# Gathers held to TensorE's progress, and table high parts copied into PSUM, in a DLRM tower kernel on one core

## The chip, the core and the metric

The kernel runs on one core of a Trainium2 chip. The metric is the time of one execution on the device, in microseconds (us). Three runs of the kernel before took 646.27, 646.14 and 642.51 us: the median is 646.14 us.

## The reference, cut to what matters

For each of 2048 samples, 27 embedding rows of 128 floats are looked up, all pairs of them are multiplied, and 351 dot products and 16 dense inputs go through three small layers:

```python
e = jnp.stack([tbl_0[ids[:, 0]], ..., tbl_26[ids[:, 26]]], axis=1)      # 2048 x 27 x 128
dot = jnp.einsum('bnd,bmd->bnm', e, e)
z = dot.reshape(2048, 27 * 27)[:, pairs]                                  # 351 pairs
h = jnp.concatenate([z, dense_ctx], axis=1)
h = jnp.maximum(h @ W_top1 + b_top1, 0.0)                                 # 367 -> 512
h = jnp.maximum(h @ W_top2 + b_top2, 0.0)                                 # 512 -> 256
y = h @ W_top3                                                            # 256 -> 1
```

All is float32. Eight tables have 1000 rows, ten 1250, eight 12500 and one 125000.

## The kernel before, in words

The batch is cut into 16 tiles of 128 samples, and four tiles make a supertile (n = 0 to 3, t = 0 to 3; tile number k = 4n + t). Embedding rows come on two ways.

**Lookups.** Ten small tables ("hot", numbers h = 0 to 9, 84 chunks of 125 rows in all) lie in SBUF, split into a high part (`table_hi`, float32r) and a low part (`table_lo`, what is missing from the high part). VectorE makes a one-hot matrix for each chunk and 512 samples (L478), and TensorE multiplies the chunk's high and low part by it (L664, L666). It does so at the head of each supertile for all four tiles, in a ring of four one-hots, and counts each chunk in the semaphore `onehot_used`. An eleventh table (HALF) is looked up in the same way in supertiles 0 and 1 (L681, L682), and gathered in 2 and 3. In supertile 0 the tables also have to be made: ScalarE copies the raw table to `table_hi` (`split_high`, L527), VectorE subtracts it from the raw table into `table_lo` (`split_low`, L444), one table ahead of its one-hots, and ScalarE copies looked-up rows from PSUM to `eT` (L582), without which TensorE can't reuse the bank two tables later.

**Gathers.** The other 16 tables ("cold"; 17 in supertiles 2 and 3) are gathered by GpSimd (POOL) with one indirect DMA for each tile and table (L434, 128 rows of 512 bytes), 264 in all, in the order of the tiles. The rows of a tile go to one of three buffers, so the gathers of tile k wait, in groups of four tables, only until TensorE has transposed the same group of tile k - 3 (semaphore `transposed`).

**Tiles.** For each tile TensorE transposes the gathered rows group by group (L692), between the groups does layer 1 of the tile two back (L723), then layer 2 of the tile three back (L745), then the products of all pairs of the tile in four PSUM banks (L710, counted bank by bank in `dot_done`), with layer 3 (L766) between. VectorE and ScalarE copy transposed rows to `eT` (L494, L574) and products to `dots` (L231). SyncE stores them to DRAM and loads them back as pairs. All these matmuls are plain float32, and the trace has two records for each matmul of L710, L723 and L745; the lookups are float32r, with one record each.

Each engine works through its own list in the order of the code. Before the change `ps_tr` (2), `ps_dot` (2), `ps_h1` and `ps_h2` are six PSUM banks of their own.

Of the kernel before, what the change touches and what calls it, by code (L numbers as in the profile page):

```python
# [16 lines left out]
P = 128  # L17
BATCH = 2048
NF = 27
ST = 4  # L20
NS = BATCH // (ST * P)
# [8 lines left out]
NH, NC = len(HOT), len(COLD)  # L30
# [4 lines left out]
CR = 125  # L35
CHUNKS = [TABLE_ROWS[f] // CR for f in TABLES]
FROM = [sum(CHUNKS[:h]) for h in range(NT + 1)]
NCH = FROM[NH]
# [15 lines left out]
M1, M2 = H1 // P, H2 // P  # L54
# [4 lines left out]
SC = P // 2  # L59
WN = 2 * NF  # L60
SG = 32
BS = 8
NB_DOT = SG // BS
# [4 lines left out]
TG = 4  # L68
# [10 lines left out]
NHALF = 2  # L79
# [5 lines left out]
LAG2 = 3  # L85

STORED = 16 * (4 + 2)
assert ST == 4 and LAG1 < LAG2 < ST and NCH % NO == 0 and NH % 2 == 0 and NX == 10 and NGX == BACK + 1 == NG - 1


def pair_rows():
# [16 lines left out]
def dlrm_tower(nc, x):  # L108
    fp32, f32r, i32 = mybir.dt.float32, mybir.dt.float32r, mybir.dt.int32
# [3 lines left out]
    with ExitStack() as ctx:  # L113
# [3 lines left out]
        def ps(name, shape):  # L117
            return ctx.enter_context(nc.psum_tensor(name, shape, fp32))
# [8 lines left out]
        table_hi = sb("table_hi", [CR, FROM[NT], P], f32r)  # L127
        table_lo = sb("table_lo", [CR, FROM[NT], P], f32r)
# [23 lines left out]
        scratch = [nc.dram_tensor(f"dots_scratch{i}", (SR, P), fp32, kind="Internal").ap() for i in range(2)]  # L152

        ps_hot = [ps(f"ps_hot{i}", [P, ST * P]) for i in range(2)]
        ps_tr = [ps(f"ps_tr{i}", [P, TG, P]) for i in range(2)]
        ps_dot = [ps(f"ps_dot{i}", [P, ST * P]) for i in range(2)]
        ps_h1 = ps("ps_h1", [P, M1, P])
        ps_h2 = ps("ps_h2", [P, 4, P])


        last_h1 = [ps_hot[0][:, 0:P], ps_hot[1][:, 0:P], ps_tr[0][:, 0, :], ps_tr[1][:, 0, :]]
        last_h2 = [ps_dot[0][:, 0:P], ps_h1[:, 0, :]]
# [64 lines left out]
            return 2 * tile(n, t) + k // 2  # L227

        def copy_products(copy, i, k):
            of = banks[k][:, 0:BS * WN].rearrange("p (g w) -> p w g", w=WN)  # L230
            return copy(dots[i][:, :, BS * k:BS * k + BS], of)  # L231


        def gathered_before(n):
# [16 lines left out]
        def groups_through(n, g):  # L251
            return groups_before(n) + g + 1
# [28 lines left out]
        def splits(h, part=1):  # L281
            return part + 1 if h == 0 else h + 2

        def in_table(table, h, part):
            a, b = part_of(h, part)
            return table[:, FROM[h] + a:FROM[h] + b]
# [127 lines left out]
        @block.gpsimd  # L414
        def _(pool):
            pool.iota(row_number[:, 0, :], pattern=[[1, CH]], base=0, channel_multiplier=KINDS[0],
                      allow_small_or_imprecise_dtypes=True).then_inc(row_number_ready, 1)
            pool.iota(row_number[:, 1, :], pattern=[[1, CH]], base=0, channel_multiplier=KINDS[1],
                      allow_small_or_imprecise_dtypes=True).then_inc(row_number_ready, 1)
            pool.memset(ident[:, :], 0.0).then_inc(ident_zero, 1)  # L420
            pool.wait_ge(ident_zero, 1)
            pool.affine_select(out=ident[:, :], in_=ident[:, :], compare_op=ALU.not_equal, fill=1.0, base=0,
                               pattern=[[-1, P]], channel_multiplier=1).then_inc(ident_ready, 1)
            for k in range(NS * ST):
                n, t = k // ST, k % ST
                if k in (0, ST):
                    pool.wait_ge(cold_ids_ready[k // ST], 16)

                n0, t0 = (k - NR) // ST, (k - NR) % ST
                for f in range(NC if gathered(n) else NC - 1):  # L430
                    g = f // TG
                    if f % TG == 0 and n0 >= 0 and g < groups(n0):
                        pool.wait_ge(transposed[t0], groups_through(n0, g))
                    pool.indirect_dma_start(  # L434
                        out=rows[k % NR][:, f, :], out_offset=None, in_=x["cold"][f][:, :],
                        in_offset=bass.IndirectOffsetOnAxis(ap=cold_ids[:, k, f:f + 1], axis=0),
                    ).then_inc(rows_ready[t][g // BACK], 16)

        @block.vector
        def _(dve):  # L440
            def split_low(h, part=0):
                a, b = part_of(h, part)
                dve.wait_ge(hi_ready, splits(h, part))
                dve.tensor_tensor(in_table(table_lo, h, part), staging[h][:, a:b], in_table(table_hi, h, part),  # L444
                                  ALU.subtract).then_inc(lo_ready, 1)


# [58 lines left out]

            for i in range(2):
                dve.memset(zT[i][96:P, 1, :], 1.0).then_inc(cleared, 1)

            for i in range(2):  # L510
                dve.memset(ps_dot[i][:, :], 0.0).then_inc(cleared, 1)
            dve.wait_ge(row_number_ready, 2)
            supertile(0, first=True)
            for n in range(1, NS - 1):
# [8 lines left out]
        def _(act):  # L523
            def split_high(h, part=0):
                a, b = part_of(h, part)
                act.wait_ge(raw_ready[h] if h else first_ready[part], 32)
                act.copy(in_table(table_hi, h, part), staging[h][:, a:b]).then_inc(hi_ready, 1)  # L527

            def half_out(n, c):
                act.wait_ge(half_onehot_used, halves(n, c) + NX)  # L530
# [121 lines left out]
        def _(pe):  # L652
# [42 lines left out]
            def products(n, t, q, first):  # L695
                if q == 0:
# [2 lines left out]
                        pe.wait_ge(hot_read[pair], hot_uses(n + 1, pair))  # L699
                    if not gathered(n):  # L700
                        pe.wait_ge(half_read, 2 * n + t // 2 + 1)
                if first and t == 0 and q == 1:
                    pe.wait_ge(cleared, 4)
                for k in (2 * q, 2 * q + 1):
                    if not (first and t == 0):
                        pe.wait_ge(dot_read[k % 2], bank_reads(n, t, k) - 1)
# [146 lines left out]
```

## Time and profile before

| | |
|---|---|
| median of three runs | 646.14 us |
| the profiled execution, its time | 642.85 us |
| the profiled execution, its span (first to last instruction) | 641.0 us |
| TensorE busy, matmuls | 404.4 us (63%) |
| VectorE busy | 215.7 us (34%) |
| ScalarE busy | 97.9 us (15%) |
| GpSimd busy | 260.6 us (41%), 259.7 of it in 264 gathers |
| granted TensorE clock, mean | 0.787 of full speed |

The profile gives for every engine when it worked and what ended its waits. "issue" in it is time in which an engine waited for nothing that the profile shows, and "remote" is a release that the profile can't place. The stages of the span, read from the timeline: lookups of supertile 0 to about 60 us and its tiles to 194; lookups of supertile 1 to 235 and its tiles to 358; lookups of supertile 2 to 398 and its tiles to 521; lookups of supertile 3 to 561 and its tiles to 623; the rest is the end of the last tile's layers.

### The profile page before, as it was taken

Reading aid. Unit: us, or ns where it says so; the run is one execution under the profiler, and the core shown is the slowest. Engines: PE = TensorE matmul, PEld = TensorE weight load, DVE = VectorE, ACT = ScalarE, POOL = GpSimd, SP = SyncE. Lnnn points to the kernel's source line nnn. Section 1 sums busy time; section 2 is a strip of 40 time slices with the busy share of each in tenths; the row PEclk is TensorE's granted clock in tenths of the full one; section 3 lists DMA queues with packets and bytes.
Section 4 is the critical chain, followed back from the end, with each engine's and each line's share of the span. In section 5 each row is a group of like instructions: output and inputs, shape, how many; then the busy total and the mean of one; then the engine's idle time right before and its main releaser. Section 6 shows DMA issues by size and latency. Waiting matters only on the chain.

```text
span 641.0 us, 9183 instructions
## 1 busy us (share of the span) xinstructions
PE 404.4 (63%) x3768; PEld 341.8 (53%) x3768; DVE 215.7 (34%) x462; ACT 97.9 (15%) x190; POOL 260.6 (41%) x272
## 2 busy tenths in 40 slices
PE   5888315263739992819271999371808089955997
PEld 3667204152628891718161888261707078845996
DVE  6898003010109960301010797010101059801220
ACT  2442001010111210102020212010201012110322
POOL 6778763544540027363645001737273600072000
PEclk9899557585959996758685999666767579985999
DMA  8983313131414202223222230123232325010322
GB/s 224 248 213 93 82 49 69 49 81 38 97 37 91 61 13 53 55 67 62 61 62 60 49 103 8 50 44 86 39 84 45 77 34 114 9 50 23 59 48 36
DMA packets 71137, 45.23 MB, mean 71 GB/s; under 512 B 53100, under 2 KB 59628, under 8 KB 71096
## 3 DMA queue, kind: packets, MB, share of 16 engines
q1 hardware_dynamic: 60578, 25.80, 18.0%
q0 software_dynamic: 8448, 17.32, 10.7%
q10 hardware_dynamic: 2070, 1.53, 1.0%
q8 instruction: 30, 0.49, 0.3%
q14 instruction: 11, 0.09, 0.0%
HBM read 38.75 MB, written 5.87 MB: 70 GB/s over the span
## 4 chain that ended last, share of the span: by engine, by line
PE 54%; issue 33%; DVE 4%; another core or an unknown queue 3%; DMA 3%; SPq 1%; ACT 1%; ACTq 0%
PE ps_hot L710 12%; PE ps_hot L664 10%; PE ps_hot L666 9%; PE ps_h L723 6%; PE ps_dot L710 6%; PE ps_tr L692 5%; PE ps_h L745 3%; DVE onehot L478 3%; DMA dots<-in_tbl 2%; PE ps_h L766 2%; PE ps_hot L681 1%; PE ps_hot L682 1%; DVE table_lo L444 1%; DMA dots_scratch<-dots 1%
## 5 line engine op out<-in xcount | busy, mean ns | idle before, releaser
L434 POOL DMA_INDIRECT rows<-in_tbl,cold_ids x264 | 259.7, 984 | 320.6 <-PE ps_tr L692 237.9
L710 PE MATMUL ps_hot<-eT 128*54 128x54 f32 x1024 | 77.2, 261 | 214.7 <-issue 195.3
L710 PEld LDWEIGHTS ps_hot<-eT 128*54 128x54 f32 x1024 | 59.1, 171 | 232.5 <-issue 211.9
L478 DVE TENSOR_SCALAR onehot<-hot_ids,row_number 125x512 fp32r<-125x512 int32 x336 | 146.8, 485 | 4.7 <-PE ps_hot L666 2.6
L664 PE MATMUL ps_hot<-onehot,table_hi 125*128 125x512 f32 x336 | 134.2, 399 | 14.8 <-DVE onehot L478 10.9
L666 PE MATMUL ps_hot<-onehot,table_lo 125*128 125x512 f32 x336 | 132.9, 396 | 0.0
L231 DVE COPY dots<-ps_hot 128x432 f32<-128x432 f32 x16 | 9.7, 608 | 238.3 <-remote 131.7
L664 PEld LDWEIGHTS ps_hot<-onehot,table_hi 125*128 125x128 f32 x336 | 64.2, 191 | 33.1 <-issue 17.6
L666 PEld LDWEIGHTS ps_hot<-onehot,table_lo 125*128 125x128 f32 x336 | 64.2, 191 | 13.1
L494 DVE COPY eT<-ps_tr 128x512 f32<-128x512 f32 (+1 forms) x36 | 23.3, 648 | 111.6 <-remote 56.4
L723 PE MATMUL ps_h<-zT,w 128*128 128x128 f32 x360 | 50.6, 281 | 0.0
L723 PEld LDWEIGHTS ps_h<-zT,w 128*128 128x128 f32 x360 | 46.0, 197 | 0.1
L582 ACT COPY eT<-ps_hot 128x512 f32<-128x512 f32 x40 | 26.6, 665 | 107.0 <-PE ps_hot L666 107.0
L692 PE MATMUL ps_tr<-ident,rows 128*128 128x128 f32 x264 | 41.8, 280 | 0.9 <-ACT eT L574 0.7
L710 PEld LDWEIGHTS ps_dot<-eT 128*54 128x54 f32 x1024 | 37.4, 164 | 6.2 <-issue 6.1
L710 PE MATMUL ps_dot<-eT 128*54 128x54 f32 x1024 | 39.4, 249 | 1.2 <-issue 1.2
L544 ACT ACTIVATE h<-ps_h,b 128x128 f32<-128x128 f32 x30 | 9.4, 363 | 159.5 <-remote 146.8
L692 PEld LDWEIGHTS ps_tr<-ident,rows 128*128 128x128 f32 x264 | 31.3, 144 | 3.3 <-ACT eT L574 1.4
L574 ACT COPY eT<-ps_tr 128x512 f32<-128x512 f32 (+1 forms) x36 | 20.1, 559 | 65.0 <-remote 39.1
L745 PE MATMUL ps_h<-h,w 128*128 128x128 f32 x240 | 29.4, 276 | 0.4 <-ACT results L554 0.4
L745 PEld LDWEIGHTS ps_h<-h,w 128*128 128x128 f32 x240 | 28.0, 192 | 0.8 <-ACT h L539 0.7
L231 DVE COPY dots<-ps_dot 128x432 f32<-128x432 f32 x16 | 9.7, 608 | 44.4 <-PE ps_dot L710 44.4
(39 smaller groups left out, 140.0 us busy)
## 6 DMA issues: line engine op xcount, KB each, us to landing
hot_ids<-in_hot_ids SPq DMA_DIRECT2D x40, 256.0 KB
dots_scratch<-dots SPq DMA_DIRECT2D x62, 87.8 KB
rows<-in_tbl,cold_ids POOLq DMA_INDIRECT x264
zT<-dots_scratch SPq DMA_DIRECT2D x47, 58.5 KB
w<-in_tbl SPq DMA_DIRECT2D x3, 448.0 KB
dots<-in_tbl SPq DMA_DIRECT2D x2, 560.0 KB
dots<-in_tbl SPq DMA_DIRECT2D x2, 448.0 KB
w<-in_tbl SPq DMA_DIRECT2D x1, 560.0 KB
```

The costliest lines, as they stand in the source:

```text
L231: return copy(dots[i][:, :, BS * k:BS * k + BS], of)
L434: pool.indirect_dma_start(out=rows[k % NR][:, f, :], out_offset=None, in_=x["cold"][f][:, :], in_offset=bass.IndirectOffsetOnAxis(ap=cold_ ...
L478: dve.tensor_scalar(onehot[:, c % NO, :], hot_ids[h % NI][0:CR, :], row, None, ALU.is_equal).then_inc(onehot_ready, 1)
L494: dve.tensor_copy(eT[:, i, :, at:at + len(f), :], ps_tr[1][:, 0:len(f), :].rearrange("d f (q b) -> d q f b", b=2))\
L574: act.copy(eT[:, t % 2, :, at:at + len(f), :], ps_tr[0][:, 0:len(f), :].rearrange("d f (q b) -> d q f b", b=2)).then_inc(tr_read[0], 1)
L582: act.copy(eT[:, :, :, NC + h:NC + h + NH + 1:NH, :], ps_hot[h % 2][:, :].rearrange("d (a i q b) -> d i q a b", a=2, i=2, b=2))\
L664: pe.matmul(ps_hot[h % 2][:, :], table_hi[:, c, :], onehot[:, c % NO, :], start=(c == FROM[h]), stop=False)
L666: pe.matmul(ps_hot[h % 2][:, :], table_lo[:, c, :], onehot[:, c % NO, :], start=False, stop=(c == FROM[h + 1] - 1)).then_inc(onehot_used, 1)
L692: last = pe.transpose(ps_tr[pair][:, f - TG * g, :], rows[tile(n, t) % NR][:, f, :], ident[:, :])
L710: last = pe.matmul(banks[k][SC * c:SC * c + WN, WN * g:WN * g + WN], e.rearrange("d a b -> d (a b)"), e.rearrange("d a b -> d b a"), start ...
L723: last = pe.matmul(ps_h1[:, m, :], w1[0:k, c, m * P:(m + 1) * P], zT[i][0:k, c, :], start=(c == 0), stop=(c == KC - 1))
L745: last = pe.matmul(ps_h2[:, m, :], w2[:, c, m * P:(m + 1) * P], h1[:, c, :], start=(c == 0), stop=(c == M1 - 1))
```

## The change

**Gathers.** A planner, `within_reach`, runs before the program is built. It counts in steps, lets gathers follow each other at 3 steps each and TensorE do a chunk in 1 step (1.3 in supertile 0) and a tile in 23 (12 for the first two), and notes for every group of gathers how many chunks and how many product banks TensorE is planned to have finished 24 steps before the group begins. GpSimd then waits for that many (`onehot_used`, `dot_done`) ahead of the group, besides the wait for `transposed` that was there.

**PSUM.** For the tables 1 to 9 and the HALF table, ScalarE also copies the raw table, rounded in the same way, to three adjoining PSUM banks (`apart`), and `hi_ready` is counted only after that copy. VectorE's subtraction reads the high part there instead of in `table_hi`. From table 3 on ScalarE waits ahead of the copy until VectorE has subtracted the table two before, which had the same banks. For this the six banks become two tensors of three banks each. The two memsets of `ps_dot` and TensorE's wait for them go, and the copies of products read only the 118 partitions that are written.

```diff
+FIRST_CHUNK, HALF_STEPS, TILE_STEPS, FIRST_TILE, BANK_STEPS, GATHER_STEPS = 1.3, 5, 23, 12, 2, 3
+FIRST_LOOKUP, FIRST_GATHER, LANDING, LEAD = 15, 9, 5, 24
...
+def within_reach():
+    begun, landed = {}, []
+    step = FIRST_GATHER
+    for k in range(NS * ST):
+        for f in range(NC if k // ST >= NHALF else NC - 1):
+            begun.setdefault((k, f // TG), step)
+            step += GATHER_STEPS
+        landed.append(step + LANDING)
+    chunks, banks = [], []
+    step = FIRST_LOOKUP
+    for n in range(NS):
+        for c in range(NCH):
+            step += 1 if n else FIRST_CHUNK
+            chunks.append(step)
+        for t in range(ST):
+            if n < NHALF and t % 2 == 0:
+                step += HALF_STEPS
+            step = max(step, landed[ST * n + t]) + (FIRST_TILE if n == 0 and t < 2 else TILE_STEPS)
+            banks += [step - BANK_STEPS * (NB_DOT - 1 - b) for b in range(NB_DOT)]
+    return {at: [sum(done <= begin - LEAD for done in of) for of in (chunks, banks)] for at, begin in begun.items()}
...
+                    if f % TG == 0 and reach[k, g][0] > chunks_done:
+                        chunks_done = reach[k, g][0]
+                        pool.wait_ge(onehot_used, chunks_done)
+                    if f % TG == 0 and reach[k, g][1] > banks_done:
+                        banks_done = reach[k, g][1]
+                        pool.wait_ge(dot_done, banks_done)
...
-                dve.tensor_tensor(in_table(table_lo, h, part), staging[h][:, a:b], in_table(table_hi, h, part),
+                high = apart[h % 2][:, 0:CHUNKS[h]] if h else in_table(table_hi, h, part)
+                dve.tensor_tensor(in_table(table_lo, h, part), staging[h][:, a:b], high,
...
-                act.copy(in_table(table_hi, h, part), staging[h][:, a:b]).then_inc(hi_ready, 1)
+                high = act.copy(in_table(table_hi, h, part), staging[h][:, a:b])
+                if h:
+                    if h > 2:
+                        act.wait_ge(lo_ready, splits(h - 2))
+                    high = act.copy(apart[h % 2][:, 0:CHUNKS[h]].bitcast(f32r), staging[h])
+                high.then_inc(hi_ready, 1)
...
-            for i in range(2):
-                dve.memset(ps_dot[i][:, :], 0.0).then_inc(cleared, 1)
...
-                if first and t == 0 and q == 1:
-                    pe.wait_ge(cleared, 4)
```

What the planner gives, worked out from its code (chunk numbers within the supertile, 84 in each):

| group of gathers | waits for |
|---|---|
| tile 0 group 3, tiles 1 and 2, tile 3 group 0 | chunk 4 (13, 23, ... 78, 84) of supertile 0 |
| tile 3 groups 1, 2, 3 | 3rd bank of tile 0; 3rd, 4th bank of tile 1 |
| tile 4 groups 0, 1; tile 5 group 0 | 1st, 4th bank of tile 2; 2nd bank of tile 3 |
| tile 5 group 1 to tile 7 group 0 | chunk 8 (20, 32, ... 80, 84) of supertile 1 |
| tile 7 group 2; tile 8 groups 0, 2, 4; tile 9 group 0 | 4th bank of tiles 4, 5, 6; 2nd, 3rd bank of tile 7 |
| tile 9 group 1 to tile 10 group 3 | chunk 11 (23, 35, ... 74, 84) of supertile 2 |
| tile 11 groups 0 to 4; tile 12 groups 0, 1, 4; tile 13 group 0 | banks of tiles 8, 8, 9, 9, 10; 10, 10, 11; 11 |
| tile 13 group 1 to tile 14 group 3 | chunk 11 (23, ... 74, 84) of supertile 3 |
| tile 15 groups 0 to 4 | banks of tiles 12, 12, 13, 13, 14 |

GpSimd's list, at the gathers of the tiles 0 to 3 (each row is a gather or a run of them, with the semaphores that it waits for). Before, 48 gathers stand with no wait but that for the ids:

```order
L434 DMA rows<-in_tbl,cold_ids 128x128 [waits cold_ids_ready0]
L434 DMA rows<-in_tbl,cold_ids 128x128 x47
L434 DMA rows<-in_tbl,cold_ids 128x128 [waits transposed0]
L434 DMA rows<-in_tbl,cold_ids 128x128 x3
L434 DMA rows<-in_tbl,cold_ids 128x128 [waits transposed0]
```

Of the change, at the end of tile 2's gathers and in tile 3's and 4's:

```order
L474 DMA rows<-in_tbl,cold_ids 128x128 [waits onehot_used]
L474 DMA rows<-in_tbl,cold_ids 128x128 x3
L474 DMA rows<-in_tbl,cold_ids 128x128 [waits onehot_used,transposed0]
L474 DMA rows<-in_tbl,cold_ids 128x128 x3
L474 DMA rows<-in_tbl,cold_ids 128x128 [waits dot_done,transposed0]
L474 DMA rows<-in_tbl,cold_ids 128x128 x3
L474 DMA rows<-in_tbl,cold_ids 128x128 [waits dot_done,transposed0]
L474 DMA rows<-in_tbl,cold_ids 128x128 x3
L474 DMA rows<-in_tbl,cold_ids 128x128 [waits dot_done,transposed0]
L474 DMA rows<-in_tbl,cold_ids 128x128 x3
L474 DMA rows<-in_tbl,cold_ids 128x128 [waits dot_done,transposed1,cold_ids_ready1]
```

No gather has changed its place; from here on a group also waits for a chunk or for a bank of products.

ScalarE's list at the tables 2 to 5 in supertile 0, before:

```order
L527 CAST table_hi<-w 125x1024 [waits raw_ready2]
L527 CAST table_hi<-w 125x1024 [waits raw_ready3]
L582 COPY eT<-ps_hot 128x128x2x2 [waits onehot_used]
L527 CAST table_hi<-dots 125x1024 [waits raw_ready4]
L582 COPY eT<-ps_hot 128x128x2x2 [waits onehot_used]
```

And of the change, in which the tensors with names in `ps_tr_h` and `ps_dot_h` are the two threes of banks:

```order
L565 CAST table_hi<-w 125x1024 [waits raw_ready2]
L569 CAST ps_tr_h<-w 125x1024
L565 CAST table_hi<-w 125x1024 [waits raw_ready3]
L569 CAST ps_dot_h<-w 125x1024 [waits lo_ready]
L625 COPY eT<-ps_hot 128x128x2x2 [waits onehot_used]
L565 CAST table_hi<-dots 125x1024 [waits raw_ready4]
L569 CAST ps_tr_h<-dots 125x1024 [waits lo_ready]
L625 COPY eT<-ps_hot 128x128x2x2 [waits onehot_used]
```

Between a table's first copy and the next copy to `eT` there is now a second copy of the table's size.

## Rows read from the trace of the kernel before

**Rows 1.** The page's span in 40 slices, digits in tenths: GpSimd, granted clock.
```profile
POOL 6778763544540027363645001737273600072000
PEclk9899557585959996758685999666767579985999
```
**Rows 2.** Waits: engine, tile, line, releaser: us in total, times, longest.
```profile
POOL rows L434 <- PE ps_tr L692: 237.9, 12, 50.8
...
PEld ps_hot L710 <- issue: 211.9, 159, 16.5
```
**Rows 3.** Gathers (L434) by stretch: length, busy (count), PE clock, DMA share, GB/s.
```profile
11.00:58.00 47.00, 37.86 (x31) 0.96 0.80 193
62.00:194.00 132.00, 69.71 (x74) 0.64 0.27 65
194.00:235.00 41.00, 0.00 (x0) 1.00 0.25 59
236.00:358.00 122.00, 62.64 (x67) 0.71 0.24 57
...
398.00:521.00 123.00, 63.71 (x68) 0.67 0.24 57
...
561.00:591.00 30.00, 16.04 (x17) 0.66 0.14 38
592.00:623.00 31.00, 0.00 (x0) 1.00 0.31 56
```
**Rows 4.** Timeline (start, us, what) of TensorE in tiles 13 to 15.
```profile
599.72 1.88 PE L710 MATMUL ps_dot<-eT 128*54 128x54 f32 x64
...
601.53 0.66 PE L692 MATMUL ps_tr<-ident,rows 128*128 128x128 f32 x4
...
612.18 0.66 PE L692 MATMUL ps_tr<-ident,rows 128*128 128x128 f32 x4
```
**Rows 5.** Timeline of all engines in tile 9, while tile 12 is gathered.
```profile
428.14 0.94 POOL L434 DMA_INDIRECT rows<-in_tbl,cold_ids  x1 [9.68 <-PE ps_tr L692]
...
430.12 0.69 DVE L494 COPY eT<-ps_tr 128x512 f32<-128x512 f32 x1 [1.52 <-PE ps_tr L692]
...
434.91 0.59 ACT L574 COPY eT<-ps_tr 128x512 f32<-128x512 f32 x1 [5.30 <-remote]
...
445.25 0.29 DVE L494 COPY eT<-ps_tr 128x128 f32<-128x128 f32 x1 [14.43 <-remote]
...
448.11 0.94 POOL L434 DMA_INDIRECT rows<-in_tbl,cold_ids  x1 [0.30 <-issue]
...
456.16 2.74 PE L710 MATMUL ps_dot<-eT 128*54 128x54 f32 x64
```
**Rows 6.** Timeline in supertile 0's lookups, gathers running.
```profile
42.33 3.25 DVE L478 TENSOR_SCALAR onehot<-hot_ids,row_number 125x512 fp32r<-125x512 int32 x8
...
43.63 1.28 POOL L434 DMA_INDIRECT rows<-in_tbl,cold_ids  x1 [0.30 <-issue]
...
43.97 0.39 PE L664 MATMUL ps_hot<-onehot,table_hi 125*128 125x512 f32 x1
...
44.42 0.40 PE L664 MATMUL ps_hot<-onehot,table_hi 125*128 125x512 f32 x1
```
**Rows 7.** Supertile 2's lookups: length, PE, PEld, DVE, ACT, POOL busy, clock, DMA.
```profile
358.00:397.00 39.00, 38.64 (x175) 31.92 (x172) 36.91 (x84) 6.76 (x11) 0.00 (x0) 1.00 0.24 63
```
**Rows 8.** Timeline: a gather beside a subtraction of `split_low`.
```profile
11.62 2.41 POOL L434 DMA_INDIRECT rows<-in_tbl,cold_ids  x1 [0.30 <-issue]
...
11.91 1.22 DVE L444 TENSOR_TENSOR table_lo<-dots,table_hi 125x1024 fp32r<-125x1024 f32 x1
```
**Rows 9.** Timeline of ScalarE and TensorE at table 3 of supertile 0.
```profile
22.32 1.05 ACT L527 CAST table_hi<-dots 125x1024 fp32r<-125x1024 f32 x1 [4.45 <-DMA dots<-in_tbl]
23.27 0.61 ACT L582 COPY eT<-ps_hot 128x512 f32<-128x512 f32 x1
...
23.98 0.47 PE L664 MATMUL ps_hot<-onehot,table_hi 125*128 125x512 f32 x1 [1.86 <-ACT eT L582]
```

More of the change, by code:

```diff
@@ L154, in dlrm_tower @@
         ps_hot = [ps(f"ps_hot{i}", [P, ST * P]) for i in range(2)]
[L155 to L158, printed above, removed]
+        ps_tr_h1 = ps("ps_tr_h1", [P, 3, 4, P])
+        ps_dot_h2 = ps("ps_dot_h2", [P, 3, 4, P])
+        apart = [bank.rearrange("p a c d -> p (a c) d")[0:CR] for bank in (ps_tr_h1, ps_dot_h2)]
+        ps_tr = [ps_tr_h1[:, i] for i in range(2)]
+        ps_dot = [ps_dot_h2[:, i].rearrange("p c d -> p (c d)") for i in range(2)]
+        ps_h1 = ps_tr_h1[:, 2]
+        ps_h2 = ps_dot_h2[:, 2]
         last_h1 = [ps_hot[0][:, 0:P], ps_hot[1][:, 0:P], ps_tr[0][:, 0, :], ps_tr[1][:, 0, :]]
@@ L229, in copy_products @@
         def copy_products(copy, i, k):
-            of = banks[k][:, 0:BS * WN].rearrange("p (g w) -> p w g", w=WN)
-            return copy(dots[i][:, :, BS * k:BS * k + BS], of)
+            of = banks[k][0:SC + WN, 0:BS * WN].rearrange("p (g w) -> p w g", w=WN)
+            return copy(dots[i][0:SC + WN, :, BS * k:BS * k + BS], of)
         def gathered_before(n):
@@ L423, in _ @@
                                pattern=[[-1, P]], channel_multiplier=1).then_inc(ident_ready, 1)
+            reach = within_reach()
+            chunks_done = banks_done = 0
             for k in range(NS * ST):
```

## The prediction

> **What bounds the kernel now.** I read four views, in this order. The slices of the page first: GpSimd's gathers and the granted clock run against each other. Where GpSimd shows no digit, the clock is at 9 (2.4 GHz); where it shows 5 to 7, the clock is at 5 to 7, half of the slice at 1.2 GHz [rows 1]. The first slices are the exception, and matter below. Then the waits: TensorE's weight loads for the products sat idle for 211.9 us for nothing that the profile shows, and GpSimd sat idle for 237.9 us until TensorE had transposed [rows 2]. So neither is busy throughout, and each waits for the other. Third, the gathers by stretch: 74, 67, 68 and 17 of the 264 lie in the tile stages of the four supertiles, none in the lookups of supertiles 1 to 3, 38 (264 less these 226) ahead of tile 0 [rows 3]. With three row buffers, tile k's gathers can only start when tile k - 3 is being transposed, and then all 16 or 17 go out in one run.
>
> Last, single tiles. Tiles 13 to 15, with no gather left, follow each other at 612.18 - 601.53 = 10.65 us [rows 4]. The four tiles of supertile 2 took 123 us [rows 3], 30.8 each. What happens in between is seen in tile 9 [rows 5]: the first gather of the run goes out at 428.14, VectorE still gets its transposed rows at 430.12, but ScalarE gets the next ones only at 434.91 (5.3 us idle), VectorE the last at 445.25 (14.4 us idle), though TensorE's records for them lie far earlier. The last gather starts at 448.11, and the second half of the products then runs at its usual pace. So while gathers are under way TensorE's float32 work nearly stands still, and the tile stages cost four clean tiles plus a price per gather: (123 - 4 x 10.65) / 68 = 1.18 us, about the step at which gathers follow each other (0.94 + 0.30 us, rows 5). This is a correlation, with no cause that the trace shows; I take it as the mechanism since tile 12, which has gathers but no ids to load for a next supertile, also took 30 us [rows 3].
>
> The lookups don't suffer so. In supertile 0 gathers run all the time, and yet chunks follow at 44.42 - 43.97 = 0.45 us [rows 6], and 84 chunks at that step are the 39 us of a later lookup stage without gathers [rows 7]. Gathers under lookups are free, and gathers under tiles cost 1.18 us each. The span is set by how many lie where.
>
> The Trainium skill's page "SBUF — State Buffer", section "Who interferes with whom", says that TensorE never waits on anyone at SBUF and that DMA doesn't contend with a compute engine. By that rule the gathers are not the cause and moving them would bring nothing; the tiles with and without them, 30.8 against 10.65 us, speak against it here.
>
> **The gathers' new waits.** They move nothing in GpSimd's list but hold groups back, from tile 5 on, until TensorE is in its next lookups. Counting what fits there: gathers beside lookups follow at 47 / 31 = 1.52 us [rows 3]. Supertile 1: held until chunk 8, so 76 chunks of 0.455 us and a half lookup of 2.5 us (estimated from the chunk's step) are left, 37 us: 24 gathers. Supertiles 2 and 3: until chunk 11, 33 us: 22 each. The planner wants 28, 25 and 25; the rest runs over into the tiles. Ahead of tile 0 I put 41 instead of 38 (next part). That makes 109 under lookups and 155 under tiles, where there were 226: 71 fewer x 1.18 = **-84 us**. Behind a waiting gather only gathers are queued on GpSimd, and TensorE waits for them last. Tile 15's last group is held until the second bank of tile 14; it lands some us later, when tile 15 has its first three groups to do. I price that at 0 to 4 us, and at 0.
>
> Two costs stand against it. The last four tiles: before, 17 gathers were done in tile 12 and three tiles ran at the 2.4 GHz level. Now 22 and more are spread over tiles 12 to 14. The gathers are in the count, but the clock isn't: 64 records of products took 2.74 us after a stall and 1.88 at full clock [rows 4, 5]. Two such halves and a layer 2 of about 1.9 us more (estimated: twice its time at half the clock) are 3.6 us a tile, three tiles: **+11 us**. And the runs are broken up: some 20 instead of 13. A run's stall sets in 2 to 3 us after its first gather, and ends some 3 us after the last [rows 5], so each further run costs 0 to 1.2 us: **+2** of at most 9.
>
> **The PSUM part.** Per table one more ScalarE copy of 1.05 us, ahead of the copy to `eT` that TensorE waits for at table 3 [rows 9]: +1 us there and about +1 for VectorE's wait at table 2 (the same 1.05 us). Later ScalarE has the time: three copies are 2.8 us beside 4.5 us of VectorE per table (eight one-hots 3.25 and a subtraction 1.22, rows 6 and 8). **+2 us.** VectorE's subtraction with one operand in PSUM isn't in the trace. Its copies out of PSUM lie at 0.69 us for 512 elements [rows 5], the subtraction at 1.22 for 1024 [rows 8], per element 1.35 against 1.19 ns with the fixed part in it. So between nothing and 10 x 0.16 = 2 us; I take 0. What it gives: the gather at 11.62 took 2.41 instead of 0.94 us beside a subtraction [rows 8]. Ten subtractions, up to 1.4 us each, are up to 14 us; those that meet a gather at half of that are 4 to 5 us, three gathers earlier, and these are the 41 above. The memsets lie ahead of the first table's arrival: 0.
>
> The same section of the skill says that a VectorE instruction with two SBUF inputs contends with a GpSimd instruction that reads SBUF; rows 8 agree, 2.41 us.
>
> **Sum.** 641.0 - 84 + 11 + 2 + 2 = 572 us of span. The profiled execution's time was 1.9 us above its span, and the median of the runs 3.3 above that; with about half of the latter, since runs scatter from 642.5 to 646.3, the predicted time is **575 us**.
>
> **Rivals.**
> - *Gathers slow the lookups too (slower).* If a gather beside f32r lookups costs TensorE as much as beside a tile, the 71 moved ones bring 71 x 1.18 = 84 us back and the costs stay: 659 us, 2% slower. It decides from 1.0 us per moved gather on. Against it rows 6: 0.45 us per chunk with gathers under way. For it only that supertiles 1 to 3 have never shown it. 4%.
> - *Gathers take VectorE's time in the lookups.* VectorE is busy for 36.91 of 39 us there [rows 7]; if each gather kept it from working for its own 0.94 us, 68 gathers are 64 us less 7 us of slack: 632 us. Against it: eight one-hots in 3.25 us with gathers beside them [rows 6]; there the gathers gave way (1.28 instead of 0.94). 4%. The skill's section has it as an exclusive lock that whoever starts first holds for the whole instruction; that would be this rival.
> - *The gathers aren't the cause.* Something else in the tile stages stalls TensorE and the new waits are nearly free: 646 us and 2 more, no change. Against it tiles 12 and 13, which differ in gathers and in time [rows 3, 4]. 3%.
> - *Short groups stall TensorE less.* The stall sets in only 2 to 3 us after a first gather; if groups of four between product banks cost 0.9 instead of 1.18 us each, 155 x 0.28 = 43 us less: 532 us. Against it that a stall also ends late. 10%.
> - The forecast, 79%, by itself 545 to 605: 155 gathers at 1.0 to 1.37 us.
>
> **How the numbers follow.** The likeliest case gives 575. The range 540 to 610 leaves out the 4, 4 and 3% above it, half of the 10% below, and little of the forecast's own: some 17%. A difference of about 1% is what a measurement of this kernel can tell from none. Faster by over 1%: 79 + 10 + 4 = 93%; within 1%: 3%; slower: 4%.
>
> **What the profile after would show.** Gathers by stretch: about 20 to 28 in the lookups of supertiles 1 to 3, which still last 39 us (wrong in the first two rivals, 50 us and more), and about 35 to 50 in each of the first three tile stages, 20 to 28 in the last. Tile stages of 85 to 95 us in supertiles 1 and 2 instead of 122. Tiles 13 to 15 longer than 10.65 us, with the clock at 5 to 8. "issue" idle time on L710 down by a third or more. GpSimd's waits now end on product banks and chunks. The first lookup stage ends 1 to 3 us later, and no gather in it takes over 2 us. I am wrong if the price per gather beside tiles, reckoned as above, isn't near 1.18, or if TensorE comes to wait for rows ahead of its transposes.

## The result, and the profile after

The changed kernel took 513.65 us (median of 4 runs, 505.62 to 516.37), the kernel before beside it 645.14 us (4 runs, 642.51 to 646.27). The ratio is 0.792, with a 95% interval of 0.783 to 0.801: 21% faster. I had forecast 575 us and a range of 540 to 610, so the direction was right and the size far off. The profiled execution has a span of 503.8 us, 137.2 less than before.

One thing has to stand ahead of all that follows. The experiments were run in six sessions. In three of them the kernel before took 382 to 386 us instead of 640, and in this second condition the traces show no loss of TensorE to gathers. Unless said otherwise, numbers are from the condition of the profile of before.

The page's slices after, GpSimd and the granted clock. Before, they ran against each other [rows 1]; now GpSimd has work in every slice but the last two, and the clock is at 9 for most of it:

```profile
POOL 6767765525426776245246676553754676554200
PEclk9959997959579999779879999998958999978999
```

The waits after, with the columns of [rows 2]:

```profile
POOL rows L474 <- PE ps_hot L751: 52.9, 10, 8.5
PEld ps_hot L751 <- issue: 52.0, 40, 18.1
...
POOL rows L474 <- PE ps_dot_h L751: 50.6, 13, 9.1
```

TensorE's unexplained idle time ahead of the products in the `ps_hot` banks fell from 211.9 to 52.0 us (with the other two banks from 218.0 to 70.6). GpSimd's long wait for the transposes (237.9 us) became shorter ones, most of them for product banks. The gathers by stretch, lookups and tiles in turn, with the columns of [rows 3]:

```profile
11.00:72.00 61.00, 45.62 (x43) 0.92 0.72 173
72.00:144.00 72.00, 34.05 (x37) 0.75 0.34 82
144.00:192.00 48.00, 29.74 (x28) 0.94 0.38 87
192.00:266.00 74.00, 31.15 (x33) 0.84 0.29 65
266.00:310.00 44.00, 31.16 (x29) 1.00 0.43 97
310.00:384.00 74.00, 36.78 (x39) 0.86 0.30 69
384.00:434.00 50.00, 34.31 (x32) 1.00 0.42 91
434.00:487.00 53.00, 17.91 (x19) 0.90 0.28 58
```

The tile stages fell from 132, 122 and 123 us to 72, 74 and 74. For an exact account I cut both traces at two kinds of record: the end of a supertile's last lookup matmul, and the end of its last product. So cut, the tiles took 135.6, 125.7, 124.4 and 63.1 us before and 76.2, 79.1, 75.2 and 57.6 after: 160.7 less, with 228 gathers starting in them before and 139 after. The lookups took 58.0, 38.7, 38.8 and 39.1 us and now 66.4, 44.9, 42.7 and 44.5: 23.9 more. All tables of tiles below are cut in this way, from one tile's last product to the next one's.

### The profile page after: what moved, and what is told of

Its sections match the earlier page's. It is cut to its first block, busy times and chain, and to the rows that moved or that the text cites. A ratio compares the mean times of both kernels' runs of the same rounds, so it can differ in the third digit from the quotient of the medians.

```text
span 503.8 us, 9238 instructions
## 1 busy us (share of the span) xinstructions
PE 390.6 (78%) x3768; PEld 328.0 (65%) x3768; DVE 218.1 (43%) x460; ACT 107.5 (21%) x200; POOL 267.1 (53%) x272
## 4 chain that ended last, share of the span: by engine, by line
PE 66%; issue 17%; another core or an unknown queue 6%; DVE 6%; DMA 3%; ACT 2%; ACTq 0%; SPq 0%; DVEq 0%
PE ps_hot L707 15%; PE ps_hot L709 14%; PE ps_hot L751 9%; PE ps_dot_h L751 7%; PE ps_tr_h L764 7%; PE ps_tr_h L735 6%; PE ps_dot_h L786 5%; DVE onehot L519 4%; PE ps_dot_h L807 2%; DMA dots<-in_tbl 1%; DMA dots_scratch<-dots 1%; ACT eT L617 1%; DVE table_lo L485 1%; DVE onehot L501 1%
## 5 line engine op out<-in xcount | busy, mean ns | idle before, releaser
L519 DVE TENSOR_SCALAR onehot<-hot_ids,row_number 125x512 fp32r<-125x512 int32 x336 | 150.1, 497 | 24.8 <-PE ps_hot L709 17.8
L707 PEld LDWEIGHTS ps_hot<-onehot,table_hi 125*128 125x128 f32 x336 | 66.4, 198 | 55.3 <-issue 34.9
L751 PE MATMUL ps_hot<-eT 128*54 128x54 f32 x1024 | 45.7, 249 | 51.5 <-issue 47.5
L709 PEld LDWEIGHTS ps_hot<-onehot,table_lo 125*128 125x128 f32 x336 | 66.6, 198 | 12.2
L535 DVE COPY eT<-ps_tr_h 128x512 f32<-128x512 f32 (+1 forms) x36 | 23.3, 648 | 107.5 <-PE ps_tr_h L735 51.5
L735 PE MATMUL ps_tr_h<-ident,rows 128*128 128x128 f32 x264 | 44.9, 296 | 11.1 <-DVE eT L535 5.4
L764 PE MATMUL ps_tr_h<-zT,w 128*128 128x128 f32 x360 | 52.2, 287 | 0.0
L751 PE MATMUL ps_dot_h<-eT 128*54 128x54 f32 x1024 | 39.2, 230 | 12.5 <-issue 12.3
L764 PEld LDWEIGHTS ps_tr_h<-zT,w 128*128 128x128 f32 x360 | 47.7, 203 | 0.1
L751 PEld LDWEIGHTS ps_dot_h<-eT 128*54 128x54 f32 x1024 | 34.7, 143 | 18.8 <-issue 18.6
L735 PEld LDWEIGHTS ps_tr_h<-ident,rows 128*128 128x128 f32 x264 | 33.5, 153 | 13.9 <-issue 10.3
L263 DVE COPY dots<-ps_dot_h 118x432 f32<-118x432 f32 x16 | 9.7, 608 | 58.1 <-remote 29.3
L786 PE MATMUL ps_dot_h<-h,w 128*128 128x128 f32 x240 | 30.8, 279 | 3.5 <-issue 3.1
L786 PEld LDWEIGHTS ps_dot_h<-h,w 128*128 128x128 f32 x240 | 28.8, 194 | 4.4 <-issue 3.6
```

The costliest lines, as they stand in the source:

```text
L263: return copy(dots[i][0:SC + WN, :, BS * k:BS * k + BS], of)
L519: dve.tensor_scalar(onehot[:, c % NO, :], hot_ids[h % NI][0:CR, :], row, None, ALU.is_equal).then_inc(onehot_ready, 1)
L535: dve.tensor_copy(eT[:, i, :, at:at + len(f), :], ps_tr[1][:, 0:len(f), :].rearrange("d f (q b) -> d q f b", b=2))\
L707: pe.matmul(ps_hot[h % 2][:, :], table_hi[:, c, :], onehot[:, c % NO, :], start=(c == FROM[h]), stop=False)
L709: pe.matmul(ps_hot[h % 2][:, :], table_lo[:, c, :], onehot[:, c % NO, :], start=False, stop=(c == FROM[h + 1] - 1)).then_inc(onehot_used, 1)
L735: last = pe.transpose(ps_tr[pair][:, f - TG * g, :], rows[tile(n, t) % NR][:, f, :], ident[:, :])
```

## The experiments

### Each part alone

`gates_only` is the kernel before with the planner and GpSimd's waits for chunks and banks, and nothing of the PSUM part:

> The kernel before with the planner and GpSimd's waits alone: six banks, table_hi in SBUF and the memsets stay. Theory 1 (the gates carry the gain): within 6 us of the changed kernel's 513.7, so 508 to 525 us. Theory 2 (a good part of what I had not forecast, some 60 us, comes from the PSUM part, through the lookups of supertile 0 or what they hand on): 560 us or more.

It took 507.52 us, a ratio to the kernel before of 0.792 (0.785 to 0.798), the same as the whole change. In its trace supertile 0's lookups take 57.2 us with 36 gathers and its tiles 86.5 us with 48; with the PSUM part it is 66.4 us with 44 and 76.2 with 40. `psum_only` is the changed kernel without these waits:

> The changed kernel without the planner's waits: the PSUM copies, the three-bank tensors and the missing memsets alone. Theory 1: 640 to 650 us, at most 2 us from the kernel before, with the lookups of supertile 0 a little longer at their start and shorter where gathers took VectorE's time (the 2.41 us subtraction gap gone). Theory 2: 585 us or less.

It took 659.92 us (4 runs, 650.95 to 668.4) against 640.52 (638.83 to 644.82): 2 to 3% slower (the two shortest, 650.95 and 657.7, are 1.6 and 2.7% above), neither theory's number. The loss lies in supertile 0. Its lookups end at 90.5 us instead of 58.0, and 12 gathers fewer are left for its tiles, which take 120.3 instead of 135.6. Windows of these lookups (length; TensorE, its weight loads, VectorE, ScalarE, GpSimd busy and their counts; clock; DMA share; GB/s):

```profile
20.00:30.00 10.00, 9.36 (x34) 7.18 (x33) 8.59 (x17) 5.55 (x7) 7.73 (x8) 0.83 1.05 241
30.00:40.00 10.00, 7.18 (x18) 3.53 (x16) 4.88 (x10) 4.24 (x5) 7.87 (x8) 0.73 0.92 208
40.00:50.00 10.00, 7.81 (x15) 4.36 (x16) 4.84 (x9) 3.01 (x3) 7.56 (x9) 0.50 0.50 131
50.00:60.00 10.00, 4.49 (x8) 1.60 (x7) 1.49 (x3) 1.76 (x2) 7.56 (x9) 0.50 0.21 56
60.00:70.00 10.00, 2.44 (x4) 1.00 (x4) 1.20 (x3) 0.00 (x0) 6.38 (x7) 0.50 0.19 51
70.00:80.00 10.00, 8.41 (x20) 5.67 (x20) 7.10 (x13) 1.79 (x2) 0.00 (x0) 0.55 0.22 64
```

TensorE goes from 34 matmuls in 10 us down to 4 while the gathers keep their pace, and recovers when they end at about 69 us. So lookups can be brought nearly to a stop as well; I had called gathers under lookups free and given 4% to the opposite. What tips them over isn't shown; the later tables in this kernel (ScalarE's second copy is ahead of each) are a guess.

### Is it VectorE's idleness?

In the lookups VectorE is busy all the time and gathers follow at 1.5 us instead of 1.25. That gave a theory: gathers stop TensorE only where VectorE is idle. First the kernel before with extra work for VectorE in the tiles of supertiles 2 and 3:

```diff
...
+                for _ in range(times):
...
+                    out = onehot[:, kept_busy[0] % 2, :].rearrange("p (a b) -> p a b", a=4)
+                    dve.tensor_scalar(out, in_table(table_hi, 0, 0)[:, 0:4].bitcast(mybir.dt.float32), row_number[0:CR, 0, 0:1], None,
+                                      ALU.is_equal).then_inc(kept, 1)
...
```

> The kernel before, nothing taken out; in the tiles of supertiles 2 and 3 VectorE has extra work: a tensor_scalar of 125 x 512 from SBUF to SBUF into unused one-hot slots, as a one-hot is made, six after each of its copies to eT, six ahead of the products and six between them, 24 to 36 a tile. Theory A (TensorE stands still only where GpSimd is issuing gathers while VectorE is idle, which is why the lookups run beside gathers freely): though work was added, the tiles of supertile 2 take about as long as VectorE's work, 18 to 24 us instead of 30.8, and the whole run 25 to 50 us less than before. Theory B (the plain float32 matmuls of the tiles are what gathers stop, whatever VectorE does): the tiles of supertile 2 take 30.8 us or more, the run as long as before or longer.

It took 640.1 us, ratio 0.994 (0.990 to 0.998). But the tiles of supertile 2 were 11.4, 20.8, 47.4 and 34.9 us long, with 5, 11, 30 and 21 gathers. The first one ran like a tile without gathers. The trace shows why (timeline of GpSimd; windows as above):

```profile
405.87 1.08 POOL L434 DMA_INDIRECT rows<-in_tbl,cold_ids  x1 [0.30 <-issue]
407.25 6.43 POOL L434 DMA_INDIRECT rows<-in_tbl,cold_ids  x1 [0.30 <-issue]
413.99 1.00 POOL L434 DMA_INDIRECT rows<-in_tbl,cold_ids  x1 [0.30 <-issue]
```
```profile
407.00:410.00 3.00, 2.60 (x68) 2.23 (x67) 3.00 (x9) 0.98 (x3) 2.75 (x1) 1.00 0.09 22
410.00:413.00 3.00, 3.00 (x78) 2.63 (x75) 3.00 (x8) 1.29 (x4) 3.00 (x1) 1.00 0.03 5
413.00:424.00 11.00, 6.89 (x73) 6.35 (x73) 11.00 (x27) 1.23 (x3) 8.77 (x8) 1.00 0.39 78
424.00:427.00 3.00, 1.45 (x23) 0.90 (x19) 3.00 (x9) 0.82 (x3) 2.49 (x2) 0.83 0.68 164
```

While VectorE ran its operations without a gap, one gather took 6.43 us, and in just these 6 us TensorE ran at full speed (68 and 78 matmuls in 3 us). Then gathers flowed again. The 73 matmuls in the next 11 us prove little: of the 4.1 us in which TensorE was idle there, 3.4 were waits for VectorE's late copies. The 3 us behind them tell more: VectorE is busy throughout, and yet TensorE does only 23 matmuls, with 1.6 us of idle time in waits that the profile can't explain, after eight gathers that had flowed since 413.99 (a ninth, at 425.75, was held up again, for 4.84 us). The held gathers were paid for in the next tiles. So it seems that a busy VectorE doesn't protect TensorE from gathers that flow, and that what it brought here came from holding GpSimd up; this rests on a few microseconds of one trace.

`act_busy` put copies of the same size on ScalarE instead:

> The kernel before; in the tiles of supertiles 2 and 3 ScalarE, not VectorE, has extra copies of 125 x 512 from SBUF to SBUF, eight after each of its copies to eT and five ahead of each of its product copies, about 30 a tile. Theory A1 (what frees TensorE is VectorE's hold on what it shares with GpSimd): nothing gained, the gathers stay 1.25 us apart and the tiles of supertile 2 take 30 us or more each. Theory A2 (any busy engine beside it does): the first tile of supertile 2 takes 11 to 20 us as with the busy VectorE.

It took 671.24 us (one run). The four tiles of supertile 2 took 29.4, 31.0, 30.6 and 30.4 us with 17 gathers each, as without the extra work: theory A1's numbers. The last three tiles, without gathers, got longer (16.0, 21.1, 15.3 us), as did the lookups ahead of them (44.9 us); the loss is mostly there.

The other half of the theory was tested by taking VectorE's work out of the lookups. `no_onehots` made 8-column one-hots:

```diff
...
+                        cut = slice(0, ST * P if c < NO else 8)
+                        dve.tensor_scalar(onehot[:, c % NO, cut], hot_ids[h % NI][0:CR, cut], row, None,
...
```

> The changed kernel with the one-hots of all chunks but the first four of a supertile made only 8 columns wide instead of 512 (most of the one-hot work is left out, so VectorE is nearly idle in the lookups; TensorE and the gathers keep all of theirs). Theory A (gathers stop TensorE while VectorE is idle): the lookups of supertiles 1 to 3 with their 28 to 32 gathers get longer, by 0.6 to 1.2 us for each gather: 65 to 85 us instead of 48, 44 and 50, and the run is 60 to 110 us above the changed kernel. Theory B (it hangs on the float32 matmuls of the tiles, float32r lookups are spared): the lookups stay at 38 to 50 us and the run within 10 us of the changed kernel.

It took 512.47 us, 0.799 (0.792 to 0.806), the lookups 47.4, 42.2 and 44.5 us. But such an operation still takes VectorE 0.25 us, so it was not idle. `idle_lookups` left most of them out:

```diff
...
+                        if n >= NHALF and not kept_one(c):
+                            continue
...
```

> The changed kernel, in whose supertiles 2 and 3 VectorE makes only the first four one-hots of the lookups whole and ten others 8 columns wide; the other 70 of 84 are left out altogether, so VectorE really is idle there while TensorE and the gathers keep all their work. (With 8-column one-hots for every chunk VectorE was still at work about half of the time, so that run decided nothing.) Theory A (gathers stop TensorE where VectorE is idle, whatever TensorE computes): the lookups of supertiles 2 and 3 grow from 42.7 and 44.5 us to 60 us or more each, with the gathers in them 1.25 us apart instead of 1.5. Theory B (float32r lookups are spared as such): they stay at 38 to 46 us.

It took 508.29 us, 0.792 (0.785 to 0.799), the two lookup stages 43.9 and 45.1 us (windows as above):

```profile
266.00:310.00 44.00, 40.62 (x173) 32.81 (x173) 3.18 (x13) 6.78 (x11) 26.12 (x29) 0.96 0.41 96
387.00:432.00 45.00, 39.50 (x171) 32.23 (x172) 3.79 (x14) 6.45 (x11) 27.44 (x29) 0.97 0.35 96
```

VectorE is busy for 3 us of 44, 29 gathers run, and TensorE does all its chunks. The theory falls: an idle VectorE doesn't let gathers stop the lookups. That float32r lookups are spared as such (theory B) fits these two runs, but not `psum_only`, where they weren't.

### Does the price depend on the run of gathers?

In the changed kernel the four tiles of supertile 2 took 16.5, 16.0, 12.4 and 30.3 us with 9, 8, 5 and 17 gathers. Above a clean tile's 10.65 [rows 4] that is 0.65, 0.67, 0.35 and 1.16 us for a gather. The last tile's 17 came in one run. Windows of it (the run starts at 354.35, its last gather at 373.08), and the timeline row of TensorE's next products:

```profile
355.00:357.00 2.00, 2.00 (x21) 2.00 (x20) 0.43 (x1) 0.59 (x1) 1.39 (x3) 1.00 0.34 70
357.00:359.00 2.00, 2.00 (x21) 2.00 (x20) 0.69 (x1) 0.00 (x0) 1.69 (x2) 1.00 0.78 144
359.00:361.00 2.00, 1.59 (x15) 1.40 (x13) 0.00 (x0) 0.00 (x0) 1.39 (x3) 1.00 0.52 104
361.00:363.00 2.00, 0.00 (x0) 0.00 (x0) 0.00 (x0) 0.00 (x0) 1.48 (x2) 1.00 0.43 111
363.00:365.00 2.00, 0.00 (x0) 0.00 (x0) 0.00 (x0) 0.00 (x0) 1.60 (x2) 0.87 0.75 207
365.00:370.00 5.00, 0.00 (x0) 0.00 (x0) 0.00 (x0) 0.00 (x0) 3.78 (x5) 0.50 0.24 64
370.00:375.00 5.00, 0.00 (x0) 0.00 (x0) 0.00 (x0) 0.59 (x1) 3.11 (x4) 0.50 0.21 53
```
```profile
378.52 3.20 PE L751 MATMUL ps_hot<-eT 128*54 128x54 f32 x64 [17.93 <-issue]
```

For some 6 us the new run costs TensorE little; then it starts nothing for 17.9 us, some 4 of them after the last gather, and the clock falls to the 1.2 GHz level. Over all tile stages, with a run taken as gathers with less than 0.8 us from the end of one to the start of the next, and TensorE's matmul records counted by the age of the run they fall in:

| matmuls started per us | no gather | 0 to 2 us | 2 to 4 | 4 to 6 | 6 to 8 | 8 to 10 | 10 to 12 | over 12 |
|---|---|---|---|---|---|---|---|---|
| before | 12.2 | 8.7 | 10.9 | 7.2 | 2.3 | 1.3 | 1.1 | 1.3 |
| after | 14.3 | 12.1 | 7.9 | 10.9 | 2.9 | 1.7 | 0.2 | 1.9 |

A start is not an end, and the first 5 us may be matmuls that were started and wait; but the sum over tiles says that short runs are cheaper. `singles` gave every gather a gate by the planner, not every group of four:

```diff
-            begun.setdefault((k, f // TG), step)
+            begun[k, f] = step
...
-                    if f % TG == 0 and reach[k, g][0] > chunks_done:
+                    if reach[k, f][0] > chunks_done:
...
```

> The kernel with the gates alone, but the planner gives a gate to every gather and not to every group of four. If what a gather takes from TensorE grows with the run of gathers it stands in (0.6 us each in fours, 1.2 in seventeens, as the tiles of the changed kernel read): the tiles with 8 or 9 gathers fall from 16 to 18 us to 13 to 15 and the run to 490 to 502 us. If it is a price for each gather: within 1% of the gates alone, 502 to 513.

It took 494.67 us, 0.767 (0.760 to 0.774), 3% below the gates alone. The total is in the first theory's range; most tiles are not: those of supertiles 1 to 3 with 7 to 10 gathers took 14.4 to 19.9 us, and a tile with 18 in one run (29.3 us) was still there.

`gates_busy` is `gates_only` with half the dose of `dve_busy`'s extra work:

> The kernel with the gates alone and the extra VectorE work in the tiles of supertiles 2 and 3, at half the dose (three operations of 125 x 512 at each place, 12 to 18 a tile). Theory A: the tiles with gathers lose less to them, and what the work itself costs (6 to 8 us of VectorE a tile of 16 to 18) is hidden: 495 to 505 us. Rival: VectorE's copies come later by the work ahead of them, and the run is 515 us or more.

It took 506.58 us, 0.788 (0.783 to 0.793), the same as the gates alone: 12 to 18 operations a tile are hidden, and bring nothing. Neither range was met.

`even` drops the planner and spreads the gathers by hand, from the 37th on one gate for each:

```diff
+FREE, IN_LOOKUPS, CHUNKS_APART, IN_TILE = 36, 28, 3, [11, 9, 10, 8]
...
+            at += [("chunk", n, CHUNKS_APART * j) for j in range(IN_LOOKUPS)]
+        points = (NG if n >= NHALF else NGX) + NB_DOT
+        for t in range(ST):
+            at += [("point", n, t, points * r // IN_TILE[n]) for r in range(IN_TILE[n])]
```

> The kernel with the gates alone, but without the planner: every gather from the 37th on has a gate of its own that is near to where TensorE is. 28 in each of the lookups of supertiles 1 to 3 (one for each 3 chunks), and 11, 9, 10 and 8 for each tile of supertiles 0 to 3, at the tile's 8 or 9 points (groups of transposes, banks of products). Theory F (in a run of gathers without a pause TensorE goes on for some 5 us and then nearly stops, so short runs are cheap and runs of 16 to 18 cost 1.2 us each): no tile has a run of over 11 any more, each takes 14 to 18 us, and the run is 475 to 492 us, below the 494.7 of a gate for each gather by the planner. A price of 0.7 us for each gather however placed: tiles of 17 to 18.5 us, 490 to 500 us.

The first two times (`even`, `even_2`) the session was in the other condition. The third time it wasn't:

> As even. Where the kernel before takes 640 us: theory F (short runs of gathers are cheap, long ones dear) 475 to 492 us; a fixed price of 0.7 us for each gather 490 to 500 us. Where it takes 382 us: within 1% of it.

468.16 us (5 runs, 465.35 to 475.87) against 643.95: 0.726 (0.723 to 0.729), 8% faster than the changed kernel by the ratios, and below even theory F's range. Its tiles in supertile 2:

| tiles 8 to 11 | us, [gathers] |
|---|---|
| before | 30.3 [17], 31.8 [17], 31.3 [17], 31.1 [17] |
| after | 16.5 [9], 16.0 [8], 12.4 [5], 30.3 [17] |
| `even_3` | 16.8 [10], 17.0 [9], 16.9 [11], 17.4 [10] |

No tile of it takes over 19.4 us. A spread gather costs about 0.6 us (four tiles 68.2 us, less 42.6, by 40), one in a run of 17 1.2 us. The number of gathers isn't what differs: supertile 2 of the changed kernel has 39 in 75.2 us, that of `even_3` 40 in 68.2. In the lookups of supertiles 1 to 3, 28 gathers each, it has 42.2, 42.2 and 42.0 us, 3.3 more than before: 0.12 each.

### Rows, bytes, and the other condition

`thin_rows` and `half_rows` are the kernel before with other gathers from tile 11 on, the first with 8 of the 128 floats of each row, the second with 64 of the 128 rows. The first one's edit:

```diff
+                    of = slice(0, 8 if k >= 11 else P)
...
+                        out=rows[k % NR][:, f, of], out_offset=None, 
+                        in_=x["cold"][f] if k < 11 else x["cold"][f].rearrange("r (a b) -> (r a) b", b=8),
```

> The kernel before, but the gathers of tiles 11 to 15 fetch 32 bytes for each of their 128 rows instead of 512 (other data than the reference's); GpSimd's instructions and the number of rows stay. In the tiles of supertile 2 (8 to 11) all gathers are of this kind. Theory D (the bytes that land are what stops TensorE): these tiles fall from 31.3 us to under 20. Theory E (it is GpSimd's issuing, row by row): they stay at 29 to 32 us.

> The kernel before, but the gathers of tiles 11 to 15 fetch 64 rows instead of 128 (the other half of each buffer keeps older rows). In the tiles of supertile 2 all gathers are of this kind. Theory E1 (the stall lasts as long as GpSimd issues rows): GpSimd's 0.95 us for a gather falls to about 0.5, 17 gathers take some 13 us, and with 5 us of them free the tiles fall from 31.3 to 17 to 21 us. Theory E2 (a price of the gather as an instruction, 1.18 us each): they stay at 29 to 32 us.

Neither theory could be judged. In that session the kernel before took 381.98 us (13 runs, 379.95 to 385.16), `thin_rows` 384.46, `half_rows` 378.85 and `even` 383.17. In the next one it was the same (before 382.88 us, `thin_rows_2` 380.89, `half_rows_2` 378.95, `even_2` 382.28 with a ratio of 0.999, 0.995 to 1.003), and in the last one again:

> As thin_rows. Where the kernel before takes 640 us: theory D (the bytes that land) under 20 us for a tile of supertile 2, theory E (GpSimd's issuing, row by row) 29 to 32 us. If the undisturbed condition is brought by these two kernels and not by the time, the kernel before beside them takes 382 us a third time.

There the kernel before took 385.5 us, `thin_rows_3` 380.67 and `half_rows_3` 378.63. One thing was seen: GpSimd takes 0.90 us for a gather of 64 rows (the mean of 20 of them in `half_rows_3`) and 0.94 for one of 128, so my step from fewer rows to a shorter instruction was wrong in any case.

> The changed kernel itself beside the others. Where the kernel before takes 640 us: 508 to 518 us. Where it takes 382 us (gathers cost TensorE nothing): the gates have nothing to gain, and what is left is the PSUM part (ScalarE's ten copies ahead of the lookups of supertile 0, some 5 us longer there) and gathers that come later: 382 to 395 us.

The changed kernel took 377.1 us there (376.33 to 380.11) against 382.88: 0.988 (0.980 to 0.995), about 1% faster and below what I expected. Its page has GpSimd at work without a pause, and the clock high throughout. Below it, windows of two of its tiles, as above:

```profile
POOL 5777877777777777777777777777778777777300
PEclk9999999999999999999999999989999999999999
```
```profile
226.00:237.00 11.00, 11.00 (x194) 10.47 (x194) 2.81 (x5) 3.96 (x10) 8.51 (x9) 1.00 0.21 55
237.00:247.00 10.00, 10.00 (x185) 9.47 (x184) 2.67 (x5) 2.96 (x7) 7.57 (x8) 1.00 0.54 113
```

Nine gathers in 11 us, and TensorE loses nothing: tiles 8 and 9 took 10.5 and 10.7 us. The instructions are the same and a gather still takes 0.94 us on GpSimd. So the kernel alone doesn't make a gather dear to TensorE. Nor is it the chip by itself: the record has chip 11 for the two first sessions, at 640 us, and for the third, at 382 (the others were on chips 7, 3 and 15, at 382.88, 643.95 and 385.5). All three sessions with `thin_rows` and `half_rows` in them were in this condition, and none of the three without. That is a striking coincidence, but I don't know whether these kernels bring it about, and no run told it apart from the time of the session.

The two conditions differ in one more thing, which the lists of DMA issues show for the gathers (their count, and the median us from issue to landing where the profile knows the landings). First the changed kernel where gathers disturb, then where they don't:

```profile
rows<-in_tbl,cold_ids POOLq DMA_INDIRECT x264
```
```profile
rows<-in_tbl,cold_ids POOLq DMA_INDIRECT x264, 3.5
```

The landing times are missing because the profiler kept fewer events. Of the semaphores' updates within the span, the eleven traces with disturbed tiles hold 3078 to 3955 and the nine others 7668 to 7830. The same kernel shows it: `even_3` has 3467 and `even` 7709. And it isn't a result of the stalls: between 10 and 50 us, in the lookups of supertile 0, these two traces have 137 and 138 matmuls and 27 and 24 gathers, but 494 and 1042 updates. So recording itself may be part of what holds TensorE up in one condition, or both may come of the same cause. Every timed execution on record has a span and a granted clock beside it, so none of them is known to have run unrecorded. That gathers disturb TensorE without a profiler at work isn't shown, and "issue" waits may in part be waits whose event was lost.

## Why the prediction was right and wrong

- **Gathers under tiles bound the kernel: right.** The gates alone bring all of it (507.5 us). The rival that they aren't the cause is out for runs in this condition, and so are those in which moved gathers cost as much, or take VectorE's time: lookups stayed below 45 us in supertiles 1 to 3.
- **How many move: nearly.** I had 155 left under tiles; there were 139, since lookups took 25 to 28 each instead of 22 to 24, and 44 instead of 41 at the start. At 1.18 us, 89 fewer instead of 71 is 105 us instead of 84, so 21 us of the miss.
- **1.18 us for each gather that stays: the step that failed.** The price was read from runs of 17 and carried over to runs of 4. Measured: 160.7 us less in the tiles, of which the count explains 105; the other 56 are, reckoned in the prediction's way, a price of 0.78 instead of 1.18 for each of 139. My fourth rival named this mechanism, but put the price at 0.9 and its chance at 10%. A sign of it stood in [rows 5]: the first gather at 428.14, a copy of transposed rows still in time at 430.12. I even charged the broken runs +2 us for it, where they were the gain.
- **+11 us for the clock: wrong.** The three last tiles took 16.1, 12.7 and 11.2 us, 7.3 more than before with 13 gathers in them. At 0.35 to 0.67 for a gather (the prices above) these explain it all, and the clock was granted at 0.90, 0.87 and 1.00 in them, not at the 0.5 to 0.8 of the forecast.
- **Lookups beside gathers are free: wrong by a little.** 81 gathers made the lookups of supertiles 1 to 3 15.5 us longer, 0.19 each. Supertile 0's took 8.4 us more, where I had +2. Between 24.8 and 32.6 us of the trace its chunks came 1.5 to 3.3 us apart, against 0.4 to 0.9 before. This belongs to the PSUM part: `gates_only` took 57.2 us there, less than before. It may be a small piece of what `psum_only` shows in full.
- **The PSUM part at +2 us: right here by luck.** With the gates it makes no difference that these runs could tell (0.792 both), and in the traces two larger terms cancel: against `gates_only`, supertile 0's lookups are 9.2 us longer and its tiles, with 8 gathers fewer in them, 10.3 shorter. Alone it costs 2 to 3%, and undisturbed the whole change is 1.2% faster. As forecast (none over 2 us), the longest gather in supertile 0's lookups took 1.30 us, where 2.41 had been seen [rows 8] and `gates_only` still has 2.42.
- **Summed:** -105 for the count, -56 for the price, +24 in the lookups is -137; I had -84 + 11 + 2 + 2 = -69.
- **Readings that were too smooth.** GpSimd and the clock don't mirror each other in every slice of [rows 1]: the eleventh has a 5 beside a 9, and the 33rd a 0 beside a 7. And the second half of the products in tile 9 didn't run "at its usual pace" after the last gather: its 64 records took 2.74 us, as the prediction itself says further down, against 1.88.

The Trainium skill's page "SBUF — State Buffer", section "Who interferes with whom", says that TensorE waits on no one at SBUF. The kernel before is at odds with the plain reading of it in one condition (30.8 us for a tile with gathers, 10.65 without) and the changed kernel is in accord with it in the other (10.5 us with 9 gathers). That it is at SBUF that TensorE is held, no run shows.

What stays open: what inside the chip holds TensorE up, whether the profiler's recording takes part in it, whether rows or bytes matter, and what sets the condition. `even` together with the PSUM part, the likely best for both conditions, wasn't run.

## What to carry to other kernels

A price read from one pattern (runs of 17) holds for that pattern; before it is multiplied by a count, look at what happened at the start of a run and cost short runs by that. Where one engine's burst disturbs another, moving it away brought most here (0.79 of the time before), and spreading what is left beside the other's progress, one gate for each instruction, brought more (0.73). And measure the kernel before beside every experiment: its 382 instead of 640 us was the largest effect in this study, and a gain found in one condition (0.73 for `even_3`) can be nothing in the other (1.00 for `even`). Where two conditions differ in how many events the profiler keeps, look for a time without it before you believe that the disturbance is the kernel's.

## What the runs showed of the hardware

- In a run of back-to-back gathers TensorE goes on for some 5 us and then starts 1 to 3 matmuls per us instead of 12 to 14; in the changed kernel's tile 11 it started none for 17.9 us.
- The same kernel took 640 or 382 us in different sessions, on one chip too (chip 11). In the long condition its TensorE is stalled beside gathers, in the short one not, and the trace of the long one keeps less than half as many semaphore updates (3467 against 7709 for `even_3` and `even`).
- Beside gapless VectorE operations of 0.48 us from SBUF to SBUF a gather took 6.43 us instead of 0.94; beside copies of the same size on ScalarE gathers still took 0.94 to 0.95 (`act_busy`).
- A gather of 64 rows takes GpSimd 0.90 us, one of 128 rows 0.94.
